# Attention groups loaded by two transfers, and a group's softmax sums computed behind the next group's last row score

## The reference

```python
qkv = x @ w_qkv.T + b_qkv                                # x is layernormed before
q, k = apply_rope(q, 0), apply_rope(k, 0)                # split into heads before
scores = jnp.einsum('bhqd,bhkd->bhqk', q, k) / math.sqrt(HEAD_DIM)
scores = jnp.where(causal[None, None, :, :], scores, jnp.float32(-1e+20))
attn = jax.nn.softmax(scores, axis=-1)
out = jnp.einsum('bhqk,bhkd->bhqd', attn, v)
...
x = x + _layernorm(attention(_layernorm(x)))             # in short
x = x + _layernorm(ffn(_layernorm(x)))
```

## Time and profile before

| | |
|---|---|
| median of 3 runs | 997.25 us (995.72 to 998.17) |
| the profiled execution, own time | 999.77 us |
| its span, first to last instruction | 997.8 us |
| TensorE busy | 976.0 us (98%) |
| VectorE, GpSimd, ScalarE busy | 716.9, 473.1, 383.7 us |
| moved by DMA | 135.11 MB, 45.5% of the 16 engines' time |
| granted TensorE clock, mean | 0.997 of full speed |

### The profile page before, as it was taken

One profiled execution on the slowest core, in us unless ns is written; L12 is line 12 of the kernel. 1 busy time (PEld: TensorE's weight loads), 2 busy tenths in 40 slices (PEclk: granted clock), 3 DMA queues, 4 the chain that ended last, 5 costly groups with the idle time before them and its releaser, 6 DMA issues.

```text
span 997.8 us, 17229 instructions
## 1 busy us (share of the span) xinstructions
PE 976.0 (98%) x6315; PEld 802.3 (80%) x6315; DVE 716.9 (72%) x1967; ACT 383.7 (38%) x661; POOL 473.1 (47%) x477
## 2 busy tenths in 40 slices
PE   5999999999999999999999999999999999999997
PEld 5888898897886666666666679999999999999996
DVE  6877495775558999989999776666666666666655
ACT  6321120210137777777778662222222222222221
POOL 1455563644449999999998811111111111111110
PEclk9999999999999999999999999999999999999999
DMA  9653635348248887666665462222223332222101
GB/s 350 227 183 114 212 135 185 124 145 209 91 147 211 201 213 184 173 159 144 156 148 148 135 208 86 88 85 85 85 85 85 85 85 85 84 77 77 59 22 43
DMA packets 80852, 135.11 MB, mean 135 GB/s; under 512 B 8040, under 2 KB 47232, under 8 KB 77696
## 3 DMA queue, kind: packets, MB, share of 16 engines
q1 hardware_dynamic: 80768, 134.00, 45.5%
HBM read 93.07 MB, written 40.38 MB: 134 GB/s over the span
## 4 chain that ended last, share of the span: by engine, by line
PE 88%; DVE 5%; DMA 3%; issue 1%; POOL 1%; ACT 1%; SPq 1%; POOLq 0%; DVEq 0%
PE bank L1462 20%; PE bank L1464 20%; PE bank L1463 20%; PE bank L1566 7%; PE bank L1544 7%; PE bank L1582 7%; DMA q_t<-shift_l 2%; PE bank L1603 1%; PE bank L1742 1%; PE bank L1609 1%; DVE ln_st L1046 1%; PE bank L1552 1%; DVE xt_raw L1157 1%; DMA k_t<-k_scratch 1%; DVE turn L1096 1%
## 5 line engine op out<-in xcount | busy, mean ns | idle before, releaser
L1119 DVE CUSTOM_DVE_ANT_0 bank<-bank,row_mask 128x384 f32<-128x384 f32 (+3 forms) x512 | 234.6, 519 | 36.7 <-PE bank L1544 36.5
L714 POOL TENSOR_TENSOR ln_rs<-ln_ve,minus_half 128x1 f32<-128x1 f32 x52 | 53.1, 1021 | 346.4 <-DVE ln_mm L1055 346.4
L920 ACT ACTIVATE prob<-bank 128x512 f32<-128x512 f32 x320 | 173.6, 599 | 27.3 <-PE bank L1566 18.4
L1464 PE MATMUL bank<-wf_l,xt_h 128*128 128x384 f32 (+3 forms) x384 | 130.1, 339 | 0.0
L1462 PE MATMUL bank<-wf_h,xt_h 128*128 128x384 f32 (+3 forms) x384 | 129.8, 338 | 0.3 <-DVE z L1311 0.3
L1463 PE MATMUL bank<-wf_h,xt_l 128*128 128x384 f32 (+3 forms) x384 | 129.7, 338 | 0.0
L1462 PE MATMUL bank<-xt_h,wq_h 128*128 128x512 f32 x304 | 119.0, 391 | 0.0
L1544 PE MATMUL bank<-k_t,q_t 96*128 96x384 f32 (+3 forms) x512 | 118.0, 328 | 0.9 <-DMA k_t<-k_scratch 0.9
L1463 PE MATMUL bank<-xt_h,wq_l 128*128 128x512 f32 x304 | 118.5, 390 | 0.0
L1464 PE MATMUL bank<-xt_l,wq_h 128*128 128x512 f32 x304 | 118.4, 389 | 0.0
L783 POOL TENSOR_TENSOR key_sum<-key_sum,prob 128x512 f32<-128x512 f32 x92 | 116.6, 1292 | 0.0
(11 more groups left out here) (128 smaller groups left out, 1948.9 us busy)
## 6 DMA issues: line engine op xcount, KB each, us to landing
q_t<-q_scratch SPq DMA_DIRECT2D x32, 512.0 KB, 5.3
q_scratch<-turn_h SPq DMA_DIRECT2D x16, 512.0 KB, 2.8
q_scratch<-turn SPq DMA_DIRECT2D x16, 512.0 KB, 3.2
q_t<-q_scratch SPq DMA_DIRECT2D x32, 256.0 KB, 5.5
att_scratch<-att SPq DMA_DIRECT2D x32, 256.0 KB, 2.9
at_raw<-att_scratch SPq DMA_DIRECT2D x16, 512.0 KB, 4.1
x<-x SPq DMA_DIRECT2D x16, 512.0 KB, 4.2
out<-z SPq DMA_DIRECT2D x15, 512.0 KB, 2.9
```

The costliest lines, as they stand in the source:

```text
L714: nc.gpsimd.tensor_tensor(ln_rs[j][:], ln_ve[j][:], minus_half[:], ALU.pow).then_inc(count, 1)
L920: nc.scalar.activation(prob[n % 2][:, i, :, :].rearrange("p h q -> p (h q)"), score_bank(n, i)[:], ACT.Exp, scale=INV_SQRT_HD).then_inc(pr ...
L1119: last = nc.vector.tensor_tensor_reduce(out=row, in0=row, in1=row_mask[:, SEQ - w:SEQ], scale=1.0, scalar=LOWEST, op0=ALU.add, op1=ALU.max ...
L1464: return mm(dst, a_h, w_l, start=False, stop=stop, skip_group_check=True)
```

## The change

Three edits. Each pair is stored in three row blocks in place of two: queries as h, l, h and keys as h, h, l, which takes a third store of 512 KB, a second one of the high half, right behind the first. `load_group` then reads 96 rows of queries in one transfer and 96 rows of keys in another, in place of four. And D goes from behind R5 to the end of the step, behind R10, for the steps 1 to 29 (the steps 30 and 31 have lists of their own, which stay). ACT's `copy_sums` goes behind the exponential with index 9, again for the steps 1 to 29.

```diff
 ORDER = ("S0 R0 R1 S1 S2 V0 V1 V2 V3 T R2 R3 R4 "
-         "S3 S4 S5 R5 D S6 R6 R7 S7 R8 S8 S9 R9 R10").split()
+         "S3 S4 S5 R5 S6 R6 R7 S7 R8 S8 S9 R9 R10 D").split()
...
-                dst = q_scratch[b, p] if p < PAIRS - 1 else k_scratch[b]
+                dst, again, low = (q_scratch[b, p], 2, 1) if p < PAIRS - 1 else (k_scratch[b], 1, 2)
                 sp.wait_ge(rope_hi, 2 * k + 2)
-                sp.dma_start(dst[0].rearrange("r p t -> p r t"), turn_h[j][:].bitcast(F32)).then_inc(qk_stored[j], 16)
+                for i in (0, again):
+                    sp.dma_start(dst[i].rearrange("r p t -> p r t"), turn_h[j][:].bitcast(F32)
+                                 ).then_inc(qk_stored[j], 16)
                 sp.wait_ge(rope_lo, 2 * k + 2)
-                sp.dma_start(dst[1].rearrange("r p t -> p r t"), turn[j][:, :, 1, :]).then_inc(qk_stored[j], 16)
+                sp.dma_start(dst[low].rearrange("r p t -> p r t"), turn[j][:, :, 1, :]).then_inc(qk_stored[j], 16)
...
-                sp.dma_start(q_dst[0:2 * HD, :], q[:, cols]).then_inc(qk_loaded[s], 16)
-                sp.dma_start(q_dst[2 * HD:KROWS, :], q[0:HD, cols]).then_inc(qk_loaded[s], 16)
-                sp.dma_start(k_dst[0:HD, :], k[0:HD, :]).then_inc(qk_loaded[s], 16)
-                sp.dma_start(k_dst[HD:KROWS, :], k[:, :]).then_inc(qk_loaded[s], 16)
+                sp.dma_start(q_dst[0:KROWS, :], q[:, cols]).then_inc(qk_loaded[s], 16)
+                sp.dma_start(k_dst[0:KROWS, :], k).then_inc(qk_loaded[s], 16)
...
                 exps(n, 5)
                 if n == NG - 2:
                     shift_to_hi(n + 1)
-                if 0 < n < NG - 1:
                     copy_sums(n - 1)
-                elif n > 0:
+                elif n == NG - 1:
                     copy_values(n - 1)
                 for i in range(6, NS):
                     exps(n, i)
+                if 0 < n < NG - 2:
+                    copy_sums(n - 1)
```

More of the change, by code:

```diff
@@ L130, in build @@
 def build(nc, x, x_t, w_qkv, b_qk, b_v, w_out, b_o, w_ffn, b_ffn, cos_t, sin_t, ident_h, row_mask_h, before_h, out):
-    q_scratch = nc.dram_tensor("q_scratch", [BATCH, PAIRS - 1, 2, 2, P, SEQ], F32).ap()
-    k_scratch = nc.dram_tensor("k_scratch", [BATCH, 2, 2, P, SEQ], F32).ap()
+    q_scratch = nc.dram_tensor("q_scratch", [BATCH, PAIRS - 1, 3, 2, P, SEQ], F32).ap()
+    k_scratch = nc.dram_tensor("k_scratch", [BATCH, 3, 2, P, SEQ], F32).ap()
     v_scratch = nc.dram_tensor("v_scratch", [NT, P, VD], F32).ap()
@@ L397, in pairs_stored @@
             for j in range(2):
-                eng.wait_ge(qk_stored[j], 32 * ((last - j) // 2 + 1))
+                eng.wait_ge(qk_stored[j], 48 * ((last - j) // 2 + 1))
         def primed_after(p, i, c):
@@ L847, in rope_to_hi @@
                 if k >= 2:
-                    act.wait_ge(qk_stored[k % 2], 32 * (k // 2))
+                    act.wait_ge(qk_stored[k % 2], 48 * (k // 2))
                 for i in range(2):
@@ L1090, in rope_half @@
                 if i == 0 and k >= 2:
-                    dve.wait_ge(qk_stored[k % 2], 32 * (k // 2))
+                    dve.wait_ge(qk_stored[k % 2], 48 * (k // 2))
                 half = bank[2 + 2 * (u % 3) + i]
@@ L1534, in row_scores @@
                 if i == 0:
-                    pe.wait_ge(qk_loaded[s], 64 * (n // SLOTS + 1))
+                    pe.wait_ge(qk_loaded[s], 32 * (n // SLOTS + 1))
                     if n == 0:
```

## The result

The changed kernel takes 1023.08 us (median of 4, 1021.33 to 1023.77), against 997.43 us before: a ratio of 1.0258, interval 1.0241 to 1.0275. That is 25.7 us more, where 21.1 were forecast (1018.3 us, range 1007 to 1030). The profiled execution took 1023.77 us, its span is 1021.1 us.

A forecast was written before the change was run, and what follows sets the result against it. TensorE was taken as the bound, busy 976.0 of 997.8 us. The terms 21.1 + 2.2 − 0.3 − 1.0 − 0.9 = +21.1 us on 997.25 gave 1018.3 us, range 1007 to 1030.

The forecast's parts named there:

- Part 1: Moving D behind R10: ACT's exponential index 6 holds S9; +0.88 us a step with cast (+21.1), +0.45 without (+2.2).
- The remark that the row scores add nothing: Attention steps: earlier row scores are taken earlier, since VectorE, which frees their banks, itself waits for them; no cost.
- Part 2: Later copy of the sums on ACT, needed by V: costed at nothing, with −0.3 us at step 30.
- The two waits for exponentials at the start of step 30: TensorE at step 30: exponentials of group 29 done earlier, so about 0.3 us of these waits goes.
- Part 3: SP's queue: loads start later behind the store of the sums, but two issues replace four; −1.0 us, ends −5.0 and +5.
- the landing gets later by 0.5, the deadline by 0.88: Transfer of the maxima: lands 0.5 us later, S0' due 0.88 us later, so present waits shrink a little.
- The upper end of the range (+5): Waits for the maxima, worst case: two transfers take as long as four, costing +5 us.
- rival B: Attention: maxima come late in every step; 0.5 us in each of 28 steps costs 14 more, 1032 us; chance 0.07.
- The first load: Load of group 0: its keys are issued about 1.1 us earlier, so the 0.9 us wait goes; −0.9 us.
- Part 4: Third store in the projections, twenty times 512 KB more: cost nothing, up to +2 us, a gain excluded.
- Rival A: Attention: ACT does not hold S9, so not slower; 991.4 us, or unchanged if the waits stay; chance 0.09.
- The rule of the Trainium skill: Group loads: about 2.0 us fixed cost per transfer; two for four save about 4 us a group, sum 4 us lower.

The follow-up runs named there:

- experiment 3: The changed kernel with ACT's cast of weights moved from between index 4 and 5 to behind index 2: 1016.41 us, ratio 1.0178 to the kernel before.
- experiment 7: Changed stores and loads, D and the copy of the sums as before the change, each cast of weights done twice: 1005.90 us, ratio 1.0073.
- experiment 1: The kernel before with only the stores and loads changed, D and the copy of the sums where they stood: 995.49 us, ratio 0.9971.
- experiment 4: The changed kernel with the store of the sums put behind the loads of group n+4 on SP, steps 1 to 27: 1018.94 us, ratio 1.0203.
- experiment 8: The kernel before with the third row block stored and read, but four transfers per group, D and copy unmoved: 998.01 us, ratio 0.9991.
- experiment 6: The changed kernel with D between R8 and S8 in place of behind R10, the copy behind index 9: 1015.20 us, ratio 1.0178.
- experiment 5: Changed stores and loads, D and copy unmoved, cast of weights moved behind index 2, against the kernel before: 995.40 us, ratio 0.9978.

## Why the prediction was right, and where its sizes were off

**Part 1, the hold: right.** +0.88 us was forecast for a step with a cast and 0.86 measured, +0.45 without and 0.51 measured: 23.2 us in place of 23.3 over 29 steps. Experiments 3 and 7 show the mechanism from both sides, by taking 0.4 us off ACT's chain and by adding 0.57 to it.

The remark that the row scores add nothing was wrong. VectorE's maxima hold row scores, 12.7 us in 57 places at the weight loads. In a step with a cast these are R7 or R8, and the hold lies inside that of S8 and S9. In a step without a cast it is also R10, the last row score before D, 0.23 us. From R5 to R9 such a step takes 547.99 − 545.80 = 2.19 us, 0.99 less than before, which makes 1.42 − 0.99 = 0.43 of loss by S9; the other 0.08 of the 0.51 come behind it, at R10. VectorE works there without a gap from the split of the maxima (545.00) to the maxima of R6 (548.13), so it is a second chain, hardly shorter than ACT's. It costs most in the steps 12, 20 and 28, where the reciprocal stands in its list: they are 0.5 to 0.8 us long, against 0.3 in experiment 1.

**Part 2, the copy: right.** It starts 371.19 − 371.06 = 0.13 us behind S0', no V waits for it in a regular step, and ACT's waits for D (0.84 us) cost TensorE nothing. The two waits for exponentials at the start of step 30 did go. Its three first scores take 580.05 − 579.16 = 0.89 us up to the V block, where they took 556.27 − 555.19 = 1.08: 0.2 won of the 0.3. It does not show in the length of the step before it, 10.02 us, since S0' stood 0.51 us there for the maxima; in experiment 4 that step takes 9.48.

**Part 3, SP's queue: the term that was mis-sized.** I took −1.0 us of waits for the maxima; the long steps grew by 2.2, from 5.1 to 7.3. Where nothing waits long for the maxima they take 1.4 us with D behind R5 (experiment 1) and 2.2 with D behind R10 (experiment 4). So the waits and what follows them cost 3.7 us before and 5.1 now: +1.4 in place of −1.0. The other 0.8 are VectorE's, of part 1. The step of it that failed is the comparison "the landing gets later by 0.5, the deadline by 0.88". The loads did start 1.4 us behind S0', as forecast (362.80 against 361.39 in a regular step; 422.08 against 420.18 in the longest, where a further load stands ahead). But the saving of 1.0 us by two issues in place of four did not bring the landing forward where a further load of 580 KB stands in front: there the maxima took 6.0 us to land, not the 4.5 + 0.5 of my reckoning. And the price of a stand was not its length. Behind the longest one the clock fell to half, which doubled its cost. Experiment 4 gives the size of the whole item: 5.1 us of the profiled steps, 4.1 of the medians. The upper end of the range (+5) had room for it; the point did not. The prediction's rival B was thus real behind the five further loads (the S0' at the end of the steps 9, 10, 12, 14 and 17 wait) and before step 30, not in every step.

**The first load: half right.** The wait for the keys of group 0 is 0.4 us in the changed kernel and absent in experiment 1; −0.9 was taken.

**Part 4, the third store: right**, by experiment 8.

**Rival A fell**, since S9 is held as reckoned; the gain that it spoke of is real but small, and belongs to the loads alone. The rule of the Trainium skill that I set against the trace ("DMA: Bandwidth & Descriptors", section "Anatomy of one DMA — SWDGE (gpsimd) path", a fixed cost of some 2 us for each transfer) would have taken all waits for the maxima away. The section gives it for transfers issued by GpSimd, and these are SP's, which the prediction did not say. Experiments 1 and 8 speak for its direction: with the same bytes, four transfers in place of two bring back 2.2 us of waits. They don't show 4 us a group.

The sum as measured: 23.2 of hold, 2.2 of long steps, −1.6 before the T of step 1 (297.48 against 299.04) and −0.5 behind step 30 make the 23.3 us between the two spans. The −1.6 are no gain of the change. They stand already in the first projections: the first matmul of 512 columns starts at 27.23 us, where it started at 28.89. The profiled execution of the kernel before had a stretch of clock 0.50 there (16 to 18 us, with 0.73 and 0.92 on either side), and that of the changed kernel had none. Without it the spans would stand some 25 us apart, close to the 25.7 of the medians; the profiled execution of the kernel before was 2.3 us above its median, that of the changed one 0.7.

So the forecast was 4.6 us low. Of this, 2.4 are the queue, 0.8 VectorE's long steps, and 0.4 the keys of group 0; the rest is within the scatter.

## What to carry to other kernels

Work that fills the list of an engine is also a spacer: D seemed free to move, since nothing waited for it, but its 1.4 us gave ACT the time to empty three banks. Before moving such a block, take the distance between the last producer and the last consumer around it (here 0.23 us between index 6 and S9) and see whether the move eats it. Do it for every engine that empties banks: behind ACT's chain stood VectorE's, hardly shorter. And count the issuing engine's queue: a store that waits for a result made later holds all the loads behind it, and nothing was lost here by putting it behind them.

## What the runs showed of the hardware that I had not expected

A stand of TensorE of 1.7 us in a stretch that is otherwise packed can be followed by half the granted clock, 0.50 in place of 1.00, for about 3.4 us (432.5 to 435.9 in the changed kernel, behind 1.68 us; likewise in experiments 3 and 6, behind 1.66 and 1.74 us, each time in the one step of 12.7 to 13.0 us). Shorter stands in attention were not followed by it: 0.8 us in the kernel before, 0.9 in the changed one, 1.2 in experiment 3. Near the start of the kernel, where TensorE is not yet packed, the clock fell behind two stands of 1.40 and 0.35 us in the kernel before and of 1.25 and 0.36 us in experiments 3 and 4. It did not fall behind one of 1.25 us in the changed kernel, nor behind 1.25 and 0.26 us in experiment 5. So the length of one stand alone doesn't decide it. In the execution of 1021.33 us of the changed kernel the clock had no such stretch; whether TensorE stood as long in it isn't known. In which way the V block that follows, with its short weight loads, has a part in it was not tried. A score that waits for an exponential starts 0.06 to 0.07 us after its end (368.87 to 368.93, 367.57 to 367.64) and has about 0.1 us of its weight load laid bare (0.34 us to the next matmul, where 0.23 is the rule).
